# The start of a fused layer's third stage: the first chunk's inputs loaded first, the folded weight made in halves behind the first chunk's products

## The reference

```
# xh = layernorm(x); y: output of the scan; norm2 = a layernorm twice
x1 = x + (y + xh * D_param) @ out_proj_w.T
x2 = x1 + layernorm(x1) @ expert_w[0].T + expert_b[0]
xn = norm2(x2) * ln_scale + ln_bias
w_dec = sigmoid(xn @ Wx.T @ Ww.T + bw)
k = xn @ Wk.T;  v = xn @ Wv.T;  r = sigmoid(xn @ Wr.T)
# then a recurrence over time on k, v, w_dec, r, an output projection, and a table-driven last layer
```

## Time and profile before

| | |
|---|---|
| median of 3 runs | 8120.26 us (8118.91 to 8121.44) |
| the profiled execution | 8123.72 us, its span 8121.9 us |
| TensorE matmul, busy in the span | 7231.2 us, 89% |
| VectorE | 6749.7 us, 83% |
| GpSimd | 5820.1 us, 72% |
| ScalarE | 4754.7 us, 59% |
| third stage, first SyncE issue to the fourth stage's first | 5134.94 to 6658.53 us |
| mean granted TensorE clock in the span | 0.957 |

### The profile page before, as it was taken

The page is one execution under the profiler, slowest core; times in us unless marked ns, Lnnn a source line. Parts: engine busy times, 40 slices in busy tenths (PEclk is TensorE's granted clock), DMA queues, the critical chain, the costliest instruction groups (busy, mean ns, idle before and its releaser), DMA issues. The chain is left out here.

```text
span 8121.9 us, 217686 instructions
## 1 busy us (share of the span) xinstructions
PE 7231.2 (89%) x74510; PEld 5288.9 (65%) x74510; DVE 6749.7 (83%) x8153; ACT 4754.7 (59%) x10889; POOL 5820.1 (72%) x3400
## 2 busy tenths in 40 slices
PE   8799999999999999999999999799999988888863
PEld 4577777777777777777777777444444435555542
DVE  7799999999999999999999999423232329999976
ACT  7778778778887787888877877211111113333320
POOL 1499999999999999999999999300000006777644
PEclk9999999999999999999999999899999998888875
DMA  6500000000000000000000000212211222222224
GB/s 208 157 1 16 16 8 8 16 13 4 16 16 0 16 16 0 16 16 0 17 16 0 16 5 0 81 74 92 88 72 72 93 77 88 88 85 86 86 84 155
DMA packets 198187, 389.94 MB, mean 48 GB/s; under 512 B 26224, under 2 KB 51888, under 8 KB 186544
## 3 DMA queue, kind: packets, MB, share of 16 engines
q1 hardware_dynamic: 189088, 370.45, 13.7%
q10 hardware_dynamic: 8976, 17.83, 0.6%
HBM read 208.52 MB, written 179.70 MB: 48 GB/s over the span
## 5 line engine op out<-in xcount | busy, mean ns | idle before, releaser
L494 POOL TENSOR_TENSOR scan_hc<-scan_h,scan_cb 128x1024 f32<-128x1024 f32 x2048 | 4776.3, 2367 | 103.0 <-PE scan_y L617 81.7
L659 DVE TENSOR_TENSOR_SCAN scan_h<-scan_a,scan_carry,scan_u 128x512 f32<-128x512 f32 x4096 | 4800.3, 1256 | 15.8 <-PE scan_u L606 8.0
L553 ACT ACTIVATE scan_a<-scan_dt,scan_aneg 128x512 f32<-128x512 f32 x4096 | 2658.3, 708 | 7.4 <-ACT scan_yo L533 7.4
L606 PE MATMUL scan_u<-scan_dg,scan_v 64*128 64x128 f32 x32768 | 2379.8, 285 | 313.3 <-DVE scan_h L659 269.5
L606 PEld LDWEIGHTS scan_u<-scan_dg,scan_v 64*128 64x128 f32 x32768 | 1990.4, 187 | 793.2 <-DVE scan_h L659 556.2
L617 PE MATMUL scan_y<-scan_ident,scan_hc 128*128 128x128 f32 x16408 | 2251.8, 280 | 14.3 <-ACT scan_yo L533 9.9
L617 PEld LDWEIGHTS scan_y<-scan_ident,scan_hc 128*128 128x128 f32 x16408 | 1758.2, 140 | 272.9 <-ACT scan_yo L533 15.7
L524 ACT ACTIVATE scan_dg<-scan_half,scan_bt 128x64 f32<-128x64 f32 x4096 | 1139.0, 341 | 5.9 <-DVE scan_onward L645 5.2
L164 POOL TENSOR_TENSOR mid_r<-mid_ve,mid_half_neg 128x4 f32<-128x4 f32 x32 | 32.4, 1012 | 1288.0 <-DVE mid_ve L132 797.7
L545 ACT ACTIVATE scan_carry<-scan_h,scan_onward 128x4 f32 (+1 forms) x1008 | 302.9, 300 | 934.3 <-DVE scan_h L659 934.2
L809 DVE TENSOR_TENSOR mid_x<-mid_x,mid_pa 128x512 f32<-128x512 f32 x64 | 44.1, 688 | 432.8 <-PE mid_pa L918 432.8
(11 more groups left out here) (212 smaller groups left out, 7246.5 us busy)
## 6 DMA issues: line engine op xcount, KB each, us to landing
scratch_y<-scan_yo ACTq DMA_DIRECT2D x17, 1024.0 KB, 4.3
pre_x<-in_x SPq DMA_DIRECT2D x16, 1024.0 KB, 5.7
scratch_dt<-pre_dt SPq DMA_DIRECT2D x16, 1024.0 KB, 5.8
scratch_vr<-pre_vr SPq DMA_DIRECT2D x16, 1024.0 KB, 4.7
scan_dt<-scratch_dt SPq DMA_DIRECT2D x16, 1024.0 KB, 5.3
scan_v<-scratch_vr SPq DMA_DIRECT2D x32, 512.0 KB, 7.6
mid_yr<-scratch_y SPq DMA_DIRECT2D x16, 1024.0 KB, 7.0
mid_x<-in_x SPq DMA_DIRECT2D x16, 1024.0 KB, 8.2
```

Source lines behind the costliest of these rows:

```text
L494: pool.tensor_tensor(hc[:, q].rearrange("p n (r j) -> p n r j", j=P), h[:, q].rearrange("p n (r j) -> p n r j", j=P), cb[:, bass.ds(b * NS ...
L553: ins = act.activation(a[:, q, n, :], dt[:, par, q, :], ACT.Exp, scale=aneg[:, q, bass.ds(m * 2 + n, 1)])
L606: mm = pe.matmul(u_ps[:, q % 2, g, k * HP:(k + 1) * HP, :], v[row, par, k, q, :], dg[row, buf, k], start=True, stop=True)
L659: ins = dve.tensor_tensor_scan(h[:, q, n, :], a[:, q, n, :], u_ps[:, q % 2, :, :, n].rearrange("p g t -> p (g t)"), carry[:, q, bass.ds(m ...
```

## The change

It touches `mid_phase` alone. The semaphore `consts` becomes three: `rows_consts` for skip, ident and wout, `ffn_consts` for w0, b0, ns, nb and bw, `proj_consts` for wk, wr and wv; `fold_in` stays. SyncE issues chunk 0's y, scale and x, then these four groups (`fold_in`'s third), then chunk 1's y, scale and x. Each engine waits for the group that its next work reads. The fold is a function of TensorE that makes the quarters given to it, now in `mid_pb`: quarters 0 and 1 behind chunk 0's `attn_out`, 2 and 3 behind chunk 0's `ffn`, with a count on `folded` for each. ScalarE copies quarter by quarter behind chunk 0's `turned_h`, after the negation of bw.

```diff
@@ SyncE
-            for dst, src in ((w["wx"], wx_d), (w["ww"], ww_d)):
-                sp.dma_start(dst[:], src).then_inc(fold_in, 16)
-            loads = [(w["wout"], wout_d), (w["w0"], w0_d), (w["wk"], wk_d), (w["wr"], wr_d), (w["wv"], wv_d),
-                     (b0, b0_d.partition_broadcast(P)), (skip, skip_d.partition_broadcast(P)), (ident, ident_d), (ns, ns_d), (nb, nb_d), (bw, bw_d)]
-            for dst, src in loads:
-                sp.dma_start(dst[:], src).then_inc(consts, 16)
+            def consts():
+                for dst, src in ((skip, skip_d.partition_broadcast(P)), (ident, ident_d), (w["wout"], wout_d)):
+                    sp.dma_start(dst[:], src).then_inc(rows_consts, 16)
+                for dst, src in ((w["w0"], w0_d), (b0, b0_d.partition_broadcast(P)), (ns, ns_d), (nb, nb_d), (bw, bw_d)):
+                    sp.dma_start(dst[:], src).then_inc(ffn_consts, 16)
+                for dst, src in ((w["wx"], wx_d), (w["ww"], ww_d)):
+                    sp.dma_start(dst[:], src).then_inc(fold_in, 16)
+                for dst, src in ((w["wk"], wk_d), (w["wr"], wr_d), (w["wv"], wv_d)):
+                    sp.dma_start(dst[:], src).then_inc(proj_consts, 16)
...
                 sp.dma_start(x[:, par], xv[c]).then_inc(x_in[par], 16)
+                if isinstance(c, int) and c == 0:
+                    consts()
@@ GpSimd
-            pool.wait_ge(consts, CONSTS * 16)
+            pool.wait_ge(ffn_consts, 80)
@@ VectorE
-            dve.wait_ge(consts, CONSTS * 16)
+            dve.wait_ge(rows_consts, 48)
@@ ScalarE
-            act.wait_ge(consts, CONSTS * 16)
-            act.mul(bwn[:], bw[:], -1.0).then_inc(bwn_ready, 1)
-            act.wait_ge(bwn_ready, 1)
-
-            act.wait_ge(folded, 1)
-            act.copy(wxw[:], pa[:]).then_inc(wxw_ready, 1)
@@ ScalarE, turned_h
                     turn_steps.inc(act.copy(ht[:, q, :], pa[:, q, :]))
+                if isinstance(c, int) and c == 0:
+                    act.wait_ge(ffn_consts, 80)
+                    act.mul(bwn[:], bw[:], -1.0).then_inc(bwn_ready, 1)
+                    act.wait_ge(bwn_ready, 1)
+                    for q in range(Q):
+                        act.wait_ge(folded, q + 1)
+                        act.copy(wxw[:, q], pb[:, q]).then_inc(wxw_ready, 1)
@@ TensorE
-            pe.wait_ge(fold_in, 32)
-
-            for q in range(Q):
-                for i in range(Q):
-                    mm = pe.matmul(pa[:, q, :], w["wx"][:, i, q * P:(q + 1) * P], w["ww"][:, i, :], start=(i == 0), stop=(i == Q - 1))
-            mm.then_inc(folded, 1)
-            pe.wait_ge(wxw_ready, 1)
-            pe.wait_ge(consts, CONSTS * 16)
+
+            def fold(rows):
+
+                pe.wait_ge(fold_in, 32)
+                for q in rows:
+                    for i in range(Q):
+                        mm = pe.matmul(pb[:, q, :], w["wx"][:, i, q * P:(q + 1) * P], w["ww"][:, i, :], start=(i == 0), stop=(i == Q - 1))
+                    mm.then_inc(folded, 1)
@@ TensorE, turn_y, attn_out, ffn (each for c == 0 alone)
+                    pe.wait_ge(rows_consts, 48)
...
+                    fold(range(Q // 2))
...
+                    pe.wait_ge(ffn_consts, 80)
...
+                    fold(range(Q // 2, Q))
+                    pe.wait_ge(wxw_ready, Q)
+                    pe.wait_ge(proj_consts, 48)
```

More of the change, by code:

```diff
@@ L689, in mid_phase @@
         half_neg = sb("half_neg", [P, J]); r0 = sb("r0", [P, J]); rr = sb("rr", [P, J]); tmp = sb("tmp", [P, J])
-        consts = sem("consts"); ticks_dve = sem("ticks_dve"); half_ready = sem("half_ready"); bwn_ready = sem("bwn_ready")
+        rows_consts = sem("rows_consts"); ffn_consts = sem("ffn_consts"); proj_consts = sem("proj_consts"); ticks_dve = sem("ticks_dve"); half_ready = sem("half_ready"); bwn_ready = sem("bwn_ready")
         y_in = [sem(f"y_in{i}") for i in range(2)]
@@ L708, in mid_phase @@
         dvep_steps = Count(sem("dvep_steps"), 2 * Q)
-        CONSTS = 11
         S_X1, S_H, S_X2 = J, J + NORM_DVE, 2 * J + NORM_DVE
```

## The result

The changed kernel takes 8100.76 us (median of 15 runs, 8097.27 to 8103.82) against 8120.09 us (15 runs, 8112.9 to 8121.44) of the kernel before: 19.3 us less, ratio 0.9979 with a 95% interval of 0.9972 to 0.9986. The prediction was 8098.2 us, 22.1 us less, in a range of 8091 to 8106.

A forecast was written before the change was run, and what follows sets the result against it. TensorE bounds the loop, so an earlier start moves its end equally. Loads 17.1 us, fold 0 and clock 5.0 sum to 22.1 us off 8120.26, giving 8098.2 us, range 8091 to 8106.

The forecast's parts named there:

- The bound: Third stage's loop: TensorE busy 97.29 us of 100, so moving the loop's start moves its end by as much.
- Part 1, the loads: Head of the third stage: VectorE starts chunk 0 at 5146.7 instead of 5163.86, 17.1 us gained.
- Part 2, the fold at 0: Chunk 0's gaps behind attn_out and ffn: each half of the fold fits into 7.86 us, costing 0 us.
- Rival (d): Gap ahead of `mid_h`'s turn: fold at low clock lands on the path, 11.8 us for both halves, slower; chance 0.05.
- Part 3, the clock: Chunk 0's chain: filled gaps keep TensorE's clock up, shortening turns, ffn and first decay; 5.0 us, ends 0 and 8.5.
- the forecast's upper end of 8.5: TensorE's chain behind VectorE's start: the gain in us if all of the clock comes, against 5.0 taken.
- (a): Chunk 0's turns: turned tiles don't hold the clock, ffn and decay start low; 8100.4 to 8102.7 us, chance 0.18.
- (b): Chunk 0's chain: all of the clock comes, living through 3.5 us ahead of chunk 1's turn; 8094.7 us, chance 0.12.
- (c): SyncE's queue: loads don't land in order of issue, VectorE starts at 5152.6; 8104 to 8108 us, chance 0.10.

The follow-up runs named there:

- the 56 transposes: Changed kernel with the whole fold behind chunk 0's ffn, plus 56 identity transposes behind attn_out; stage 1507.5 us, 3.5 less than with that gap empty.

## Why the prediction was right, point by point

**The bound.** Right. The loop's waits did not change, and the 20.3 us won before chunk 1's attn_out (16.1 and 4.3) came out at the stage's end.

**Part 1, the loads: 17.1 us forecast, 16.1 measured.** The mechanism held: VectorE's first skip ended its wait on `mid_wout`, as written. (It started at 5148.57 where 5146.7 was written; 0.8 us of that is the stage's own later start, 5135.81 against 5135.02.) Too small was the time from SyncE's first issue to the landing of what is wanted, 11.6 us forecast and 12.6 measured. The issues with their times to landing (the first 13.5 us of the stage):

```profile
mid_yr<-scratch_y SPq DMA_DIRECT2D x1, 1024.0 KB, 5.1
mid_x<-in_x SPq DMA_DIRECT2D x1, 1024.0 KB, 7.2
mid_wout<-in_out_proj SPq DMA_DIRECT2D x1, 1024.0 KB, 10.0
...
mid_skip<-in_d_row SPq DMA_DIRECT2D x1, 256.0 KB, 7.8
...
mid_ident<-in_ident SPq DMA_DIRECT2D x1, 64.0 KB, 8.1
```

With the issues at 5135.93, 5136.92, 5137.39, 5137.94 and 5138.54, y landed at 5141.0, x at 5144.1, skip at 5145.2, ident at 5146.0 and wout at 5148.5. y took 5.1, not 5.5; x 3.1 more, where 2.5 to 3 was taken; wout 2.5 as taken. The miss is in the two small loads: 0.33 MB at the pace of the large ones was 0.8 us, and they took 1.9. SyncE's extra increments and wait cost 0.2 us, as taken (its first issue stands 0.12 us behind the memset, before 0.08 ahead of it). Nobody waited for the weights behind; chunk 1's skips followed its norm without a wait, at 5210.96.

**Part 2, the fold at 0.** Right to a tenth. The halves take 7.03 us each, and 0.99 and 1.09 us of waiting for VectorE are left. The turns start 7.86 and 7.95 us behind the products, as in the earlier trace rows. ScalarE's last copy ends at 5210.60 (0.58 us, not 0.51), 0.5 us ahead of the turn, where 0.2 was written. Rival (d) falls: the fold ran at full clock.

**Part 3, the clock: 5.0 forecast, 4.3 measured.** The turn of h 3.67 to 1.97 (1.70, as taken). ffn 17.00 to 15.70 (1.3, as taken from attn_out's row, though with some luck: behind the same wait of 2.14 us it took 14.00 in two of the experiments, and no row told which it would be). The turn of x against chunk 1's turn of y, 6.62 to 5.54 us (1.1, as taken), and what ends the wait is now VectorE's `mid_yr`, as written. The term that failed is the last: 0.9 us was taken for chunk 1's turn of y and the first decay, and the clock was down for both, 3.67 and 8.05 us, 0.1 us worse than before. The first turn of chunk 0 and the steps around it gave the 0.3 us that is left. In the one profile of the old order of loads the same moved fold gave 8.7 us, near the forecast's upper end of 8.5; so 4.3 us is what it gives in this kernel, and not a constant of the move. Stretches of the wait of 3.6 us and of what follows:

```profile
5213.00:5216.50 3.50, 0.01 (x1) 0.00 (x0) 3.44 (x6) 3.37 (x5) 0.00 (x0) 0.83 0.47 154
5216.50:5218.50 2.00, 1.89 (x9) 1.90 (x10) 0.00 (x0) 0.69 (x1) 0.00 (x0) 0.50 1.06 392
```

**The rivals.** (a), turns that don't hold the clock, would end where ffn stays at 17.00. The clock did fall behind the wait ahead of ffn, but only after it had been 1.00 through turn and wait, and ffn took 15.70; that the turns hold it the 56 transposes settle. (b) would need the clock through the 3.6 us wait, and it fell there; with products in that wait it came, and turn and decay gave 2.7 of that run's 4.2 us. (c) falls with the landings in the order of issue. Of the 2.8 us between the gain forecast (22.1) and the medians' difference (19.3), 1.0 is the loads, 0.7 the clock, and the rest is within the spread of the other stages.

## What to carry to other kernels

At the start of a stage, write down for each engine what its first instruction reads, and queue the loads in that order with a semaphore for each step. A setup product that stands ahead of the first chunk in an engine's own queue, and whose inputs now load later, must move as well, or the earlier loads are worth nothing, as the run with the fold at the head shows. The gaps of a lone first chunk are free room for it, and filling them also keeps TensorE's clock: in the changed kernel that gave a fifth of the whole gain.

## What the runs showed of the hardware that was not expected

- A wait of 2.14 us of TensorE's cost 1.7 us of the products behind it in some kernels (15.70 us) and nothing in others (14.00 us). The changed kernel showed 15.70 in each of three profiles; the kernels with 14.00 were profiled once each. Why is open: a clock that had been up before the wait fell after it in the changed kernel and stayed up in the kernels with the old order of loads (ffn) and with the fold at the head (attn_out).
- 6.3 us of float32 transposes held the granted clock at 1.00, and a row of 84 of them, behind 8.9 us of idling, brought it from 0.50 to 1.00.
- 256 KB broadcast to all partitions and 64 KB of identity took 1.9 us of the queue between x and wout, against 2.5 us for a load of 1024 KB.
